# Batching the statistics of the closing layer norm, two output buffers on two DMA queues, and no transposes after the last FFN

## The reference

```python
x = _layernorm(x + attn(x))      # attn: q * cumsum(k*v) * sigmoid(gate)
y = x
for l in range(2):               # _layer: local attention (8 heads of 64, window 512),
    y = _layer(y, ...)           #   then shift, LN, FFN 1024 -> 2*2730 (GELU gate) -> 1024
x = _layernorm(x + y)            # the closing norm, the part that the change rewrites
```

## Time and profile before

| | us |
|---|---|
| median of 2 runs | 4512.55 (4498.61 to 4526.48) |
| the profiled execution | 4434.34 |
| its span, slowest core (core 2) | 4432.7 |
| spans of the 8 cores | 4375.0 to 4432.7 |

### The profile page before, as it was taken

How to read it: one execution, slowest core, us unless ns; L and a number is a source line. 1 busy time by engine, 2 the same in 40 slices (tenths; PEclk the granted TensorE clock), 3 DMA queues, 4 the chain that set the end, 5 groups by cost and what they waited for, 6 DMA issues and landing times.

```text
span 4432.7 us, 35811 instructions; the slowest of 8 cores (4375.0 to 4432.7 us)
## 1 busy us (share of the span) xinstructions
PE 2856.4 (64%) x10925; PEld 1078.9 (24%) x11068; DVE 1499.0 (34%) x2252; ACT 568.0 (13%) x890; POOL 508.0 (11%) x917
## 2 busy tenths in 40 slices
PE   2655565334678786449999644487878538999920
PEld 1312121111222222113334311122222203434310
DVE  2773333243332322432222234422323322222144
ACT  0011111011111112020111010011121121100101
POOL 3000000100000000213443100000000024333200
PEclk9877776666555555769999766655555758988855
DMA  6000000200000000355765100000000056555411
GB/s 105 13 0 10 8 10 10 41 0 0 1 1 1 0 1 2 50 71 78 102 84 81 38 0 0 0 1 1 0 1 1 10 89 87 78 77 68 59 65 49
DMA packets 137383, 143.19 MB, mean 32 GB/s; under 512 B 33436, under 2 KB 115356, under 8 KB 137200
## 3 DMA queue, kind: packets, MB, share of 16 engines
q0 software_dynamic: 127840, 121.71, 19.5%
q1 hardware_dynamic: 9360, 19.17, 1.2%
HBM read 249.90 MB, written 12.58 MB: 59 GB/s over the span
## 4 chain that ended last, share of the span: by engine, by line
PE 57%; DVE 22%; issue 7%; DMA 6%; ACT 5%; POOL 2%; DVEq 1%; ACTq 0%; SPq 0%; POOLq 0%
PE pA L1013 6%; PE pG L1018 5%; PE pQKV L498 5%; PE pP L277 5%; PE pX3a L1069 4%; PE pX3b L1069 4%; PE pAV L689 3%; DVE g2f L298 2%; DMA W1g<-w_i 2%; PE pST L706 1%; PE pST L709 1%; DVE XT L163 1%; PE pS L709 1%; PE pS L706 1%; PE pWo L786 1%
## 5 line engine op out<-in xcount | busy, mean ns | idle before, releaser
L1013 PE MATMUL pA<-HN,W1a 128*128 128x512 bf16 (+1 forms) x1380 | 361.7, 406 | 77.4 <-DMA W1g<-w_i 46.2
L1018 PE MATMUL pG<-HN,W1g 128*128 128x512 bf16 (+1 forms) x1382 | 349.9, 396 | 1.6 <-issue 0.2
L1037 DVE SCALAR_TENSOR_TENSOR HG<-pA,b1ac,scr 128x512 bf16<-128x512 f32 (+1 forms) x176 | 132.0, 750 | 577.1 <-ACT scr L1032 577.1
L995 POOL DMA_DIRECT2D W1a<-w_i x384 | 238.1, 620 | 719.9 <-PE pG L1018 700.5
L751 DVE CAST Arbc<-pS 64x512 bf16<-64x512 f32 x32 | 21.8, 683 | 696.6 <-PE pS L746 696.6
L999 POOL DMA_DIRECT2D W1g<-w_i x384 | 241.3, 628 | 29.6 <-issue 29.5
L498 PE MATMUL pQKV<-AQ,XT 128*128 128x512 bf16 x748 | 234.9, 483 | 11.9 <-DVE rope L474 9.4
L1032 ACT ACTIVATE scr<-pG,b1gc 128x512 bf16<-128x512 f32 (+1 forms) x176 | 120.9, 687 | 861.6 <-PE pG L1018 748.1
L564 PE MATMUL pT<-k_cI,f16c 128*128 128x128 f16 x128 | 18.7, 300 | 329.8 <-DVE f16c L557 329.8
L769 POOL DMA_DIRECT2D AO<-wo_i x8 | 4.3, 561 | 1899.8 <-DVE AoT L754 1899.8
L277 PE MATMUL pP<-WqkvT,XT 128*128 128x512 bf16 x747 | 206.7, 422 | 2.5 <-issue 1.7
(11 more groups left out here) (237 smaller groups left out, 3689.3 us busy)
## 6 DMA issues: line engine op xcount, KB each, us to landing
W1a<-w_i POOLq DMA_DIRECT2D x320, 128.0 KB, 6.4
W1g<-w_i POOLq DMA_DIRECT2D x320, 128.0 KB, 6.8
W2i<-w_i POOLq DMA_DIRECT2D x42, 256.0 KB, 16.7
out<-of_sb SPq DMA_DIRECT2D x16, 512.0 KB, 2.6
wst<-Wqkv POOLq DMA_DIRECT2D x24, 256.0 KB, 3.6
AQ<-wqkv_i POOLq DMA_DIRECT2D x16, 384.0 KB, 14.3
XS<-x POOLq DMA_DIRECT2D x16, 256.0 KB, 15.4
x1h<-XS SPq DMA_DIRECT2D x16, 256.0 KB, 2.0
```

Of the source, the lines that this page charges most:

```text
L995: E("ge", lambda e, j=j, b5=b5, wa=wa, l=l, bb=bb: e.dma_start(out=W1a[bb][:, 512 * j:512 * j + wa], in_=self.dw1[l, 128 * j:128 * (j + 1) ...
L1013: ins = e.matmul(pA[pp][0:wh, :], W1a[bb][:, 512 * j + 128 * i5:512 * j + 128 * i5 + wh], HNc[:, 512 * j:512 * (j + 1)], start=(j == 0), s ...
L1018: ins = e.matmul(pG[pp][0:wh, :], W1g[bb][:, 512 * j + 128 * i5:512 * j + 128 * i5 + wh], HNc[:, 512 * j:512 * (j + 1)], start=(j == 0), s ...
L1037: E("ve", lambda e, wh=wh, pc=pcglob, pp=pp: e.scalar_tensor_tensor(HG[0:wh, 512 * pc:512 * (pc + 1)], pA[pp][0:wh, :], b1ac[0:wh, pc:pc + ...
```

## The change

Three things, all at the program's end:

1. `layer_ffn` runs its closing transposes for layer 0 only, and notes `self.ve_ffn_done`, DVE's count after the last L1076. `final` waits for that count where it waited for `xt_ready`.
2. The 16 loads of `x1h` are shared between SP (even tiles) and POOL (odd tiles).
3. `final` is written as passes over all tiles: an add in place in `X1L` and its row sum for each tile; the squares on ACT, in two buffers in turn, with their row sums on DVE; the small operations once, on 128x16 columns of a new tile `STT`; then the f32 results, in two buffers in turn, stored by SP (even tiles) and POOL (odd tiles).

```diff
-        ve_xt3 = {}
-        for t in range(NT):
-            w = [("ve", ve_ffn_done)]
-            if t > 1:
-                w.append(("ve", ve_xt3[t - 2]))
-            ve_xt3[t] = self.transpose_tile_to_xt(t, pX3[t % 2], w)
+        self.ve_ffn_done = ve_ffn_done
+        if l < 1:
+            ve_xt3 = {}
+            for t in range(NT):
...
+        STT = self.sb(stZ, "STT", [128, 80], F32)
+        of2 = [self.of_sb, self.sb(stZ, "of2", [128, 1024], F32)]
+        sq2 = [self.scr[1], self.scr[2]]
+        vdone = self.ve_ffn_done
...
+            if t % 2 == 0:
+                E("sy", lambda e, t=t: e.dma_start(
+                    out=X1L[:, 1024 * t:1024 * (t + 1)],
+                    in_=self.dx1h[128 * t:128 * (t + 1), :]),
+                  wait=([("dh", self.x1h_stored), ("ve", vdone)] if t == 0 else []),
+                  inc=[("dh", 16)])
+            else:
+                E("ge", lambda e, t=t: e.dma_start(
...
+                  wait=([("ve", vdone)] if t == 1 else []),
+                  inc=[("dv1", 16)], dma=True)
+        ld_all = [("dh", C["dh"]), ("dv1", C["dv1"])]
+        for t in range(NT):
             E("ve", lambda e, t=t: e.tensor_tensor(
-                s_sb[:], X1L[:, 1024 * t:1024 * (t + 1)],
-                self.XS[:, 1024 * t:1024 * (t + 1)], op=OP.add), wait=w)
-            E("ve", lambda e: e.tensor_reduce(stat[:, 0:1], s_sb[:], axis=AX.X, op=OP.add))
+                X1L[:, 1024 * t:1024 * (t + 1)], X1L[:, 1024 * t:1024 * (t + 1)],
+                self.XS[:, 1024 * t:1024 * (t + 1)], op=OP.add),
+              wait=(ld_all if t == 0 else []))
+            E("ve", lambda e, t=t: e.tensor_reduce(
+                STT[:, t:t + 1], X1L[:, 1024 * t:1024 * (t + 1)], axis=AX.X, op=OP.add))
+            ve_add[t] = C["ve"]
+        for t in range(NT):
+            par = t % 2
+            w = [("ve", ve_add[t])]
+            if t >= 2:
+                w.append(("ve", ve_redq[t - 2]))
+            E("se", lambda e, t=t, par=par: e.activation(
+                sq2[par][:], X1L[:, 1024 * t:1024 * (t + 1)], AF.Square), wait=w)
+            E("ve", lambda e, t=t, par=par: e.tensor_reduce(
+                STT[:, 16 + t:17 + t], sq2[par][:], axis=AX.X, op=OP.add),
               wait=[("se", se_sq)])
+            ve_redq[t] = C["ve"]
...
+        prev = {0: None, 1: None}
+        for t in range(NT):
+            par = t % 2
+            w = [prev[par]] if prev[par] else []
+            E("ve", lambda e, t=t, par=par: e.scalar_tensor_tensor(
+                of2[par][:], X1L[:, 1024 * t:1024 * (t + 1)], STT[:, 48 + t:49 + t],
+                STT[:, 64 + t:65 + t].broadcast_to((128, 1024)),
+                op0=OP.mult, op1=OP.add), wait=w)
             ve_o = C["ve"]
+            if par == 0:
+                E("sy", lambda e, t=t: e.dma_start(
+                    out=self.dout[128 * t:128 * (t + 1), :], in_=of2[0][:]),
+                  wait=[("ve", ve_o)], inc=[("dy", 16)])
+                prev[0] = ("dy", C["dy"])
+            else:
+                E("ge", lambda e, t=t: e.dma_start(
+                    out=self.dout[128 * t:128 * (t + 1), :], in_=of2[1][:]),
+                  wait=[("ve", ve_o)], inc=[("dv0", 16)], dma=True)
+                prev[1] = ("dv0", C["dv0"])
```

More of the change, by code:

```diff
@@ L1081, in layer_ffn @@
         ve_ffn_done = C["ve"]
-        ve_xt3 = {}
-        for t in range(NT):
-            w = [("ve", ve_ffn_done)]
-            if t > 1:
-                w.append(("ve", ve_xt3[t - 2]))
-            ve_xt3[t] = self.transpose_tile_to_xt(t, pX3[t % 2], w)
+        self.ve_ffn_done = ve_ffn_done
+        if l < 1:
+            ve_xt3 = {}
+            for t in range(NT):
+                w = [("ve", ve_ffn_done)]
+                if t > 1:
+                    w.append(("ve", ve_xt3[t - 2]))
+                ve_xt3[t] = self.transpose_tile_to_xt(t, pX3[t % 2], w)
         self.xt_ready = C["ve"]
@@ L1101, in final @@
         X1L = self.sb(stZ, "X1L", [128, NT * 1024])
-        stat = self.stat
-        s_sb, sq_sb = self.scr[0], self.scr[1]
+        STT = self.sb(stZ, "STT", [128, 80], F32)
+        of2 = [self.of_sb, self.sb(stZ, "of2", [128, 1024], F32)]
+        sq2 = [self.scr[1], self.scr[2]]
+        vdone = self.ve_ffn_done
         for t in range(NT):
[L1105 to L1109, removed]
@@ L1110, in final @@
-        dh_all = C["dh"]
-        prev_store = 0
+            if t % 2 == 0:
[6 more added lines that the diff above has]
+                E("ge", lambda e, t=t: e.dma_start(
+                    out=X1L[:, 1024 * t:1024 * (t + 1)],
+                    in_=self.dx1h[128 * t:128 * (t + 1), :]),
+                  wait=([("ve", vdone)] if t == 1 else []),
+                  inc=[("dv1", 16)], dma=True)
@@ L1112, in final @@
+        ld_all = [("dh", C["dh"]), ("dv1", C["dv1"])]
+        ve_add = {}
         for t in range(NT):
-            w = [("dh", dh_all), ("ve", self.xt_ready)]
-            if prev_store:
-                w.append(("dy", prev_store))
             E("ve", lambda e, t=t: e.tensor_tensor(
-                s_sb[:], X1L[:, 1024 * t:1024 * (t + 1)],
-                self.XS[:, 1024 * t:1024 * (t + 1)], op=OP.add), wait=w)
-            E("ve", lambda e: e.tensor_reduce(stat[:, 0:1], s_sb[:], axis=AX.X, op=OP.add))
@@ L1120, in final @@
-            ve_s = C["ve"]
-            E("se", lambda e: e.activation(sq_sb[:], s_sb[:], AF.Square),
-              wait=[("ve", ve_s)])
+                X1L[:, 1024 * t:1024 * (t + 1)], X1L[:, 1024 * t:1024 * (t + 1)],
[4 more added lines that the diff above has]
+            ve_add[t] = C["ve"]
@@ L1123, in final @@
+        ve_redq = {}
+        for t in range(NT):
[5 more added lines that the diff above has]
+                sq2[par][:], X1L[:, 1024 * t:1024 * (t + 1)], AF.Square), wait=w)
             se_sq = C["se"]
-            E("ve", lambda e: e.tensor_reduce(stat[:, 1:2], sq_sb[:], axis=AX.X, op=OP.add),
+            E("ve", lambda e, t=t, par=par: e.tensor_reduce(
+                STT[:, 16 + t:17 + t], sq2[par][:], axis=AX.X, op=OP.add),
@@ L1125, in final @@
               wait=[("se", se_sq)])
[L1126 to L1142, removed]
@@ L1143, in final @@
-            E("ve", lambda e: e.scalar_tensor_tensor(
-                self.of_sb[:], s_sb[:], stat[:, 6:7],
-                stat[:, 7:8].broadcast_to((128, 1024)), op0=OP.mult, op1=OP.add))
-            ve_o = C["ve"]
[L1147 to L1151, removed]
+            ve_redq[t] = C["ve"]
@@ new lines, in final @@
+        E("ve", lambda e: e.tensor_scalar_mul(STT[:, 32:48], STT[:, 0:16], 1.0 / D))
+        E("ve", lambda e: e.tensor_tensor(STT[:, 48:64], STT[:, 32:48], STT[:, 32:48],
+                                          op=OP.mult))
+        E("ve", lambda e: e.scalar_tensor_tensor(STT[:, 48:64], STT[:, 16:32], 1.0 / D,
+                                                 STT[:, 48:64], op0=OP.mult,
+                                                 op1=OP.subtract))
+        E("ve", lambda e: e.tensor_scalar(STT[:, 48:64], STT[:, 48:64], 1e-5, None,
+                                          op0=OP.add))
@@ new lines, in final @@
+        ve_var = C["ve"]
+        E("se", lambda e: e.activation(STT[:, 48:64], STT[:, 48:64], AF.Ln),
+          wait=[("ve", ve_var)])
+        E("se", lambda e: e.activation(STT[:, 48:64], STT[:, 48:64], AF.Exp, scale=-0.5))
+        se_rs = C["se"]
+        E("ve", lambda e: e.scalar_tensor_tensor(STT[:, 64:80], STT[:, 32:48], -1.0,
+                                                 STT[:, 48:64], op0=OP.mult,
+                                                 op1=OP.mult),
+          wait=[("se", se_rs)])
@@ L1152, in final @@
+        E("sy", lambda e: e.nop(), wait=[("dy", C["dy"]), ("dv0", C["dv0"])])
         self.b.flush(self.blk)
```

## The result

| | us |
|---|---|
| before, median of 10 runs | 4423.95 (4400.11 to 4526.48) |
| changed kernel, median of 11 runs | 4321.30 (4300.67 to 4447.62) |
| ratio | 0.9782, 95% interval 0.9752 to 0.9812 |
| profiled execution of the changed kernel | 4321.80, span 4320.2 |

I forecast 94.0 us less, 2.1%. Measured are 2.18% (1.9 to 2.5), which is 96 us of 4424. The saving was forecast to within its interval. The time was not: 4321.3 lies under the lower end of my range, 4332. The interval of the ratio crosses 0.98, so whether the gain is over 2%, where I put 0.56, is not decided by these runs. The two executions of the kernel before on which my 4512.55 rests are the slowest two of the ten. Every kernel here has a slower state in some executions, in which one die's granted clock is lower, and the ratio is of undisturbed runs.

The account below looks back on a forecast made before the run. The prediction took a chain of waits at the program's end as the bound: 22.1 us saved by the earlier start and 71.9 in the passes, 94.0 in all, so 4512.55 - 94.0 = 4418.5 us, range 4332 to 4452.

Parts of the forecast that it names:

- What bounds the kernel: Program's end, 4219.5 to 4432.7: no engine full, a chain of waits; its 213.2 us are all there is to win.
- Part 1, loads earlier: After the last add: transposes gone, DVE starts 22.1 us earlier; transfer-bound loads still take 14.3 us despite two queues.
- Part 2, passes 1 and 2: Closing norm: adds with row sums take 34.1 us, squares with row sums 21.3, both paced by DVE.
- The thin cover of the squares: Second pass: ACT's squares just covered by DVE's row sums, by 0.05 us a tile; 0.8 us if lost.
- The small operations: Between squares and results: done once on 16 columns instead of per tile, 2.0 us.
- Pass 3: Results and stores: POOL's store, landing in 3.7 us, sets rounds of 5.76 us for two tiles; 42.9 us in all.
- The end: After the last result: 0.60 to POOL's start, 3.7 landing, 0.3 to the end of the span; 4.6 us.
- The two stores slow each other: Rival in Pass 3: POOL's landing becomes 4.65 us, the round 6.71, saving 86.4 us, time 4426.1; chance 0.26.
- POOL's issue is held up by DVE: Rival in Pass 3: descriptors wait for DVE's result, 0.73 us more a round, saving 88.2 us, time 4424.4; chance 0.14.
- A store from POOL is a slow kind of transfer: Rival in Pass 3: landings up to 38.3 us make the kernel slower, 4695 us; chance 0.04.
- the bounds of the landing: POOL's store in Pass 3: landing in 2.6 us would save 102.8 us in all, in 6.1 us 74.8.

Follow-up runs that it names:

- e1: The kernel before with only layer 1's closing transposes left out; tail (end of last L1076 add to end of span) 191.5 us against 213.2.
- e3: The changed kernel with all 16 x1h loads on SP, stores untouched; tail 116.0 us against 117.2.
- e5: The changed kernel with one output buffer and all 16 stores from POOL; tail 155.1 us against 117.2.
- e8: The changed kernel with only the very last store (tile 15) moved from POOL to SP; tail 112.9 to 113.7 us on the eight cores.
- e7: The changed kernel with loads and part of the passes beside the last FFN chunk, four output buffers on SP; median 4259.1 us, 0.9629 of the kernel before.
- a2: The changed kernel unaltered, run again beside the kernel before; ratio 0.9771 (0.9701 to 0.9841), tails 116.0 to 117.2 us.
- e6: The changed kernel with four output buffers and all stores on SP; tail 97.7 us, ratio to the kernel before 0.978 (0.9732 to 0.9828).
- e2: The changed kernel with all stores on SP, two buffers, loads untouched; tail 107.6 us, single execution 4330.16 us.
- e4: The kernel before, tile by tile, with only the two output buffers and stores on SP and POOL in turn; tail 174.4 us against 213.2.

## Why the prediction was right and wrong

**What bounds the kernel: right.** The end of the kernel was a chain of waits, and the tail alone takes the measured saving, 96.0 us.

**Part 1, loads earlier: right.** Forecast 22.1 us, measured in e1 21.7, in the changed kernel 36.5 - 14.7 = 21.8 (last add to first add of the norm). That two queues would not speed the loads was shown by e3; the 14.3 us that I kept are 14.7.

**Part 2, passes 1 and 2: right.** 34.1 + 21.3 = 55.4 us forecast, 4272.74 - 4217.69 = 55.05 measured. The thin cover of the squares held. The small operations: 2.0 forecast, 2.2 measured.

**Pass 3: right mechanism, one term too dear.** I took 3.7 us for the landing of a store from POOL, from wst; it is 3.0 in the median, and 2.9 alone (e5). A round is (4312.21 - 4276.30)/7 = 5.13 us, not 5.76, and the pass 38.6 us, not 42.9. A wst load is another kind of transfer: it reads DRAM, and is converted from f32 to bf16 on its way. The DMA's rows of three single transfers show that its transfer is longer (first row busy tenths in 40 slices, second GB/s written). A wst load in the kernel before, over 4 us:

```profile
DMA  1100000200009252936999999998712100000099
GB/s 21 21 0 0 0 0 0 82 0 0 0 0 143 20 41 20 164 61 123 225 205 184 205 246 164 184 266 164 143 0 41 21 0 0 0 0 0 0 82 123
```

The last store of the changed kernel, over 6.1 us:

```profile
DMA  0000000899998995000000000000000000000000
GB/s 0 0 0 0 0 0 0 349 403 376 430 430 376 430 403 242 0 0 0 0 0 0 0 0 0 0 0 0 0 0 0 0 0 0 0 0 0 0 0 0
```

SP's first store in the kernel before, over 3 us:

```profile
DMA  0000000000019898999998999969800000000000
GB/s 0 0 0 0 0 0 0 0 0 0 0 55 492 328 492 328 437 437 437 382 492 328 437 437 382 437 273 492 328 0 0 0 0 0 0 0 0 0 0 0
```

The load moves data for about 18 slices of 0.1 us, 1.8 us, at some 200 GB/s written in the denser half of them. POOL's store takes 9 slices of 0.15, 1.4 us, at 400, and so does SP's (18 slices of 0.075). Whether direction or conversion makes the load slower no run separates. The two stores differ only in when the data starts: 1.06 us after the issue from POOL (slice 7), 0.77 from SP (slice 11), 0.3 us. The sentence that I worked out from the Trainium skill (DMA: Bandwidth & Descriptors, latency and other measured facts), 2.6 + 0.4 = 3.0, was nearer than my row, since it started from a store; the trace has 0.3 for its 0.4 (1.06 and 0.77 us to the first data). The nearer row was SP's store of the same bytes plus the difference of the queues, not a converting load of the same queue.

**The end: too short.** 4.6 us forecast from the last result, 4320.2 - 4313.5 = 6.7 measured: 0.6 and 3.0, and then 3.0 in which the program goes on after the store has landed, as it does not when the last store is SP's (e8). I took the 0.3 us of the kernel before, whose last DMA was SP's.

In all, the tail is 117.2 us where my sum had 4338.7 - 4219.5 = 119.2: pass 3 4.3 too long, the end 2.1 too short, the rest 0.2 too short. That the sum is within 2 us is luck in part: the two larger errors have opposite signs.

**The rivals.** "The two stores slow each other": they do, but not where it counts. SP's store takes 3.2 us in the median instead of 2.6, and landings of up to 4.0 us occur; POOL's, which sets the round, is 0.1 above e5's. As the term that I priced, 4.65 us in POOL's round, it fell. What it costs is inside the 2.5 us that DVE idles behind SP's stores. "POOL's issue is held up by DVE": fell with e5 by the same 0.1; the hold-up that the Trainium skill (SBUF — State Buffer, who interferes with whom) states for some VectorE operations does not show with this f32 result. "A store from POOL is a slow kind of transfer": 2.9 us.

**The step that failed** is "the range takes the bounds of the landing and the spread of the runs: from the profiled execution less 102.8 (4332)". The saving in it was right: 96.0 us, inside the bounds of 74.8 and 102.8, and 2.0 from my 94.0. The anchor was not. The spread was that of three executions, 4434.34 to 4526.48, and I took the lowest as a floor, as if no execution of the kernel before could be faster. Of the ten executions in the table above five are under 4415 us and the lowest is 4400.11, 34 us or 0.8% under my floor; less the measured 96.0 it makes 4304. The point forecast has the same fault: 4512.55 - 94.0 = 4418.5 is 97 us above the median of 4321.3, since the two executions behind 4512.55 are the slowest of the ten. The profiles show where such a difference sits. The code up to the last L1076 is the same in every kernel here but e7, and on the core that reaches its end last it ends at 4219.5 us in the kernel before, at 4203.0 in the changed kernel, at 4189.3 in a2 and between 4204.3 and 4235.8 in e1 to e6 and e8: 47 us of spread ahead of the tail, while the tail of one kernel holds within some 2 us from core to core.

What stays open: why cores and executions reach the tail so far apart (58 us from core to core in the kernel before, 75 in e5), which is the size of the miss; what happens in the 3 us at the end; and the clock of cores 4 and 5 in e7.

## What to carry to other kernels

When a chain of waits sets the end, write down the round of each buffer (work, issue, landing, return) and let the longest set the pace; the sum came out within 2 us of 117, though two of its errors cancelled in part. For the landing of a transfer that the trace lacks, start from one of the same direction, bytes and type, and correct for the queue; plain stores were cheaper on SP here, by 9.6 us (e2). Spread a saving in microseconds over more than the two or three absolute times that are at hand: the ratio was good to 0.1%, the time was not.

## What the runs showed of the hardware

- A plain 512 KB store is issued 0.55 us later after a DVE result from POOL than from SP (0.63 against 0.08) and needs 0.3 us more to its first data; the transfer is the same 1.4 us. The wst load, which reads DRAM and converts f32 to bf16, wrote some 200 GB/s in the same view, half of the 400 of a plain store.
- A program whose last DMA is POOL's ends some 3 us after it has landed (3.0, 3.6, 2.4 and 2.4 us of wait in the changed kernel, e5, e3 and e4), one whose last is SP's after 0.2 (e1, e2, e6 and e8).
- Two stores in flight slow each other, but do not queue: SP's landed in 3.2 us in the median beside POOL's, 2.6 beside another of SP's with two buffers (e2; 3.6 at most) and 3.1 with four (e6), against 2.6 alone. Four buffers still reached 377 GB/s with a result every 1.4 us.
